# Batch 0: q, k and the shift copied straight from SBUF into the stacks, head by head, and weight folding placed behind the column sums

## The reference

```python
# layer 0: 8 heads of 16, per batch
q, k, v = x @ Wq, x @ Wk, x @ Wv              # split into heads
w = softmax(where(adj > 0, q @ k.T / sqrt(16), -1e9))
x = layernorm(x + (w @ v) @ Wo + bo)
# layer 1
h = x @ W.T
e = (h @ a1)[:, None] + (h @ a2)[None, :]
e = where(e >= 0, e, 0.2 * e)
x = layernorm(x + softmax(where(adj > 0, e, -9e15)) @ h)
```

## Time and profile before

| | us |
|---|---|
| median of 3 runs | 891.87 |
| lowest, highest | 888.39, 896.82 |
| the profiled execution | 889.27 |
| span of its records | 887.3 |
| TensorE busy | 818.8 (92%) |
| ScalarE busy | 702.3 |
| VectorE busy | 698.0 |

### The profile page before, as it was taken

The page is one execution under the profiler, slowest core; times in us unless marked ns, Lnnn a source line. Parts: engine busy times, 40 slices in busy tenths (PEclk is TensorE's granted clock), DMA queues, the critical chain, the costliest instruction groups (busy, mean ns, idle before and its releaser), DMA issues.

```text
span 887.3 us, 19518 instructions
## 1 busy us (share of the span) xinstructions
PE 818.8 (92%) x7647; PEld 400.1 (45%) x7680; DVE 698.0 (79%) x1141; ACT 702.3 (79%) x766; POOL 118.1 (13%) x92
## 2 busy tenths in 40 slices
PE   6399999989999999999999999999999999998982
PEld 4023334425643365334643357333653356433861
DVE  5288679797788978988788977988878987788473
ACT  2399899999779977899779986899769996898050
POOL 4000100030012010031001120132000220122030
PEclk9599999999999999999999999999999999999997
DMA  4656617441266135452365224661363422401001
GB/s 148 147 158 174 132 62 191 152 87 49 96 175 146 39 100 128 129 124 63 106 169 149 37 78 143 156 133 37 107 166 117 90 85 85 96 2 49 1 13 39
DMA packets 51779, 92.16 MB, mean 104 GB/s; under 512 B 3729, under 2 KB 20882, under 8 KB 51666
## 3 DMA queue, kind: packets, MB, share of 16 engines
q1 hardware_dynamic: 51682, 90.85, 38.8%
HBM read 67.63 MB, written 23.20 MB: 102 GB/s over the span
## 4 chain that ended last, share of the span: by engine, by line
PE 69%; ACT 15%; issue 9%; DVE 5%; POOL 0%; POOLq 0%; ACTq 0%; DVEq 0%
PE acc L474 18%; PE slot L509 12%; ACT weights L632 11%; PE slot L441 9%; PE slot L450 9%; PE slot L520 3%; PE slot L446 3%; PE slot L453 2%; ACT atts L658 2%; PE slot L557 2%; DVE x L920 2%; PE slot L571 2%; PE slot L547 2%; PE slot L579 2%; PE slot L491 1%
## 5 line engine op out<-in xcount | busy, mean ns | idle before, releaser
L632 ACT ACTIVATE weights<-slot 128x1024 f32<-128x1024 f32 x504 | 491.8, 1040 | 75.8 <-PE slot L450 38.0
L844 DVE SCALAR_TENSOR_TENSOR weights<-mask,weights 128x1024 f32<-128x1024 bf16 x336 | 403.4, 1236 | 52.8 <-ACT weights L632 42.7
L474 PE MATMUL acc<-weights,vst 128*17 128x512 f32 x2048 | 243.6, 594 | 0.0
L441 PE MATMUL slot<-qst,kst 97*32 97x512 bf16 x2240 | 160.5, 383 | 5.8 <-ACT weights L632 5.2
L450 PE MATMUL slot<-qst,kst 97*128 97x512 bf16 x464 | 133.6, 389 | 25.7 <-issue 13.8
L509 PEld LDWEIGHTS slot<-hst,atts 128*128 128x128 f32 x896 | 106.8, 191 | 17.4 <-ACT weights L632 9.6
L509 PE MATMUL slot<-hst,atts 128*128 128x129 f32 x896 | 110.5, 276 | 3.2 <-issue 1.7
L474 PEld LDWEIGHTS acc<-weights,vst 128*17 128x17 f32 x2048 | 52.3, 97 | 119.8 <-issue 96.8
L441 PEld LDWEIGHTS slot<-qst,kst 97*32 97x32 bf16 x2240 | 49.5, 95 | 116.0 <-ACT weights L632 49.3
L859 DVE SCALAR_TENSOR_TENSOR atts<-turn,hst,mask 128x1024 f32<-128x1024 f32 x64 | 83.2, 1323 | 21.5 <-DMA k_scratch<-atts 15.2
L781 POOL TENSOR_TENSOR rstd<-vareps,exponent 128x4 f32<-128x4 f32 (+1 forms) x24 | 29.3, 1222 | 468.3 <-DVE vareps L915 468.3
(11 more groups left out here) (135 smaller groups left out, 683.5 us busy)
## 6 DMA issues: line engine op xcount, KB each, us to landing
raw<-in_adjT SPq DMA_DIRECT2D x64, 512.0 KB, 3.6
q_scratch<-atts SPq DMA_DIRECT2D x48, 256.0 KB
qst<-q_scratch SPq DMA_DIRECT2D x16, 768.0 KB
k_scratch<-atts SPq DMA_DIRECT2D x24, 256.0 KB
kst<-k_scratch SPq DMA_DIRECT2D x16, 384.0 KB
xT_sb<-in_xT SPq DMA_DIRECT2D x8, 512.0 KB, 4.4
kst<-k_scratch SPq DMA_DIRECT2D x16, 256.0 KB
x_sb<-in_x SPq DMA_DIRECT2D x8, 512.0 KB, 4.7
```

Source lines behind the costliest of these rows:

```text
L441: mm = pe.matmul(ps[rows, cols], kst[:, h, keys], qst[:, h, cols], start=True, stop=not by_pe)
L474: mm = pe.matmul(acc[VW * i:VW * i + HD + 1, cols], vst[b % 2][:, t, g * HG + i], weights[:, HG * buffer(b, n) + i, cols], start=(t == 0), ...
L632: act.activation(to, ps[:], ACT.Exp, scale=SCALE).then_inc(exp_done, 1)
L844: dve.scalar_tensor_tensor(out=to, in0=masks[b % 2][:, n % T], scalar=0.0, in1=at, op0=ALU.is_equal, op1=ALU.mult).then_inc(masked, 1)
```

## The change

For batch 0 alone, nothing goes through DRAM: first_stacks copies each block of each head with one SBUF-to-SBUF transfer (16 rows of 1024 bf16), and the shift of each head with one of a single row. The order is q part 0 and k part 0 of group 0, q parts 1 and 2, k parts 1 and 2, the shift rows of group 0; then all pieces of group 1 and its shift rows. All of it takes the place of the job partsq of batch 0; the other jobs for the parts, the shift and the stacks of batch 0 are empty. From batch 1 on all is as before, with the counts of the semaphores moved and with waits of batch 1's writers of the parts and the shift on the stacks of batch 0. In PE's program fold_second_layer moves from behind k to behind cc; q no longer waits for wk.

```diff
     STACK_DMAS = 5
+    FIRST_DMAS = (2 * BLOCKS + 1) * HG
...
+        def stacks_in(b):
+            return 16 * (FIRST_DMAS + STACK_DMAS * b)
...
                 if b > 0:
                     for g in range(NG):
-                        sp.wait_ge(stack_in[g], b * 16 * STACK_DMAS)
+                        sp.wait_ge(stack_in[g], stacks_in(b - 1))
...
+            def place(s, i, g):
+                for r in range(BLOCKS):
+                    if (QPART, KPART)[s][r] == i:
+                        for h in range(g * HG, (g + 1) * HG):
+                            sp.dma_start((qst, kst)[s][r * HD:(r + 1) * HD, h],
+                                         parts[s][i][h * HD:(h + 1) * HD]).then_inc(stack_in[g], 16)
+
+            def first_stacks():
+                for s in range(2):
+                    sp.wait_ge(part0_made, s + 1)
+                    place(s, 0, 0)
+                for s in range(2):
+                    sp.wait_ge(parts_made, s + 1)
+                    place(s, 1, 0)
+                    place(s, 2, 0)
+                sp.wait_ge(taken["cc"], 1)
+                for h in range(H):
+                    if h == HG:
+                        for s in range(2):
+                            for i in range(3):
+                                place(s, i, 1)
+                    sp.dma_start(qst[KROWS:SROWS, h], negshift[h:h + 1]).then_inc(stack_in[h // HG], 16)
...
             def job(name, me):
-                if name[:3] == "raw":
+                if me == 0 and (name[:5] in ("parts", "stack") or name == "shift"):
+                    if name == "partsq":
+                        first_stacks()
+                elif name[:3] == "raw":
...
-            sp.dma_start(wq[:], Wq).then_inc(wqk_in, 16)
+            sp.dma_start(wq[:], Wq).then_inc(wq_in, 16)
             load_xT(0)
-            sp.dma_start(wk[:], Wk).then_inc(wqk_in, 16)
+            sp.dma_start(wk[:], Wk).then_inc(wk_in, 16)
...
                 if u % (UNITS // NG) == 0:
-                    pe.wait_ge(stack_in[g], (b + 1) * 16 * STACK_DMAS)
+                    pe.wait_ge(stack_in[g], stacks_in(b))
...
                     if me == 0:
-                        pe.wait_ge(wqk_in, 32)
+                        pe.wait_ge(wq_in if name == "q" else wk_in, 16)
...
                     pe.wait_ge(squares_made, 2 * me + 2)
+                    if me == 0:
+                        pe.wait_ge(pool_step, 4)
...
                         job(name, me)
-                        if me == 0 and name == "k":
+                        if me == 0 and name == "cc":
                             fold_second_layer()
...
                 if name in ("q", "k"):
+                    if me == 1:
+                        for g in range(NG):
+                            act.wait_ge(stack_in[g], stacks_in(0))
...
                     act.wait_ge(kmax_made, me + 1)
-                    act.wait_ge(shift_out, me * 16)
+                    if me == 1:
+                        for g in range(NG):
+                            act.wait_ge(stack_in[g], stacks_in(0))
+                    if me > 1:
+                        act.wait_ge(shift_out, (me - 1) * 16)
...
                 dve.wait_ge(parts_made, 2 * b + s)
+                if b == 1:
+                    for g in range(NG):
+                        dve.wait_ge(stack_in[g], stacks_in(0))
```

More of the change, by code:

```diff
@@ L239, in build_fast @@
         acc_read = sem("acc_read")
-        wqk_in = sem("wqk_in")
+        wq_in = sem("wq_in")
+        wk_in = sem("wk_in")
         consts_in = sem("consts_in")
@@ L357, in load_stack @@
                 if what == "q":
-                    sp.wait_ge(parts_out[0], (b + 1) * 96)
+                    sp.wait_ge(parts_out[0], b * 96)
                     sp.dma_start(qst[0:KROWS, heads], q_scratch[heads].rearrange("h i d n -> (i d) h n")).then_inc(stack_in[g], 16)
                 elif what == "k":
-                    sp.wait_ge(parts_out[1], (b + 1) * 48)
+                    sp.wait_ge(parts_out[1], b * 48)
                     for r, n in K_RUNS:
@@ L365, in load_stack @@
                 else:
-                    sp.wait_ge(shift_out, (b + 1) * 16)
+                    sp.wait_ge(shift_out, b * 16)
                     sp.dma_start(qst[KROWS:SROWS, heads], shift_scratch[heads].rearrange("(o h) n -> o h n", o=1)).then_inc(stack_in[g], 16)
@@ L848, in sum_atts @@
                 if j == 0:
-                    dve.wait_ge(parts_out[0], min(b + 3, B) * 96)
-                    dve.wait_ge(parts_out[1], min(b + 3, B) * 48)
+                    dve.wait_ge(parts_out[0], (min(b + 3, B) - 1) * 96)
+                    dve.wait_ge(parts_out[1], (min(b + 3, B) - 1) * 48)
                     dve.wait_ge(full["cc"], min(b + 3, B))
```

## The result

The changed kernel takes 922.39 us (median of 4; 921.97 to 923.14) against 891.38 before: a ratio of 1.0345, 95% interval 1.0316 to 1.0374. It is 31 us slower. The forecast was 905, slower, with a range up to 916: the direction came out, and so did the wait that carries the loss; the size is over twice what was forecast, and outside the range.

What follows compares the result with a forecast made beforehand. The stack load alone was taken to hold unit 0 back, then SyncE's issue ahead of raw 2: 12.6 (mask 2) + 3.0 (clock) = +15.6 on 889.27 gives 904.9, rounded 905 us; range 885 to 916.

Steps and rivals of the forecast that it cites:

- the price of a piece: SyncE's issue of each of batch 0's 96 copies of 16 rows: 0.475 us, ends kept 0.27 and 0.65.
- the near rows: Setup loads and k stack transfers issued right behind each other on SyncE, 0.43 us long, gaps to 0.48, taken as price.
- The 0.30 for the shift's rows: SyncE's issue of each of the 8 single-row shift copies in batch 0, put at 0.30 us.
- The rest of the sum: SyncE free at 57.3, raw 2 lands at 60.9, mask 2 12.6 us later; with 3.0 for the clock, +15.6.
- The clock's term: TensorE idles ahead of mask 2, so what follows starts at 1.2 GHz: 3.0 us more, bounds 0 and 5.
- rival D: Slack later in batch 0 takes up the stall, only the earlier unit 0 stays: 886.7 us; chance 0.03.
- Unit 0: First unit of batch 0, after group 0's pieces: starts at about 35.0 instead of 37.6, 2.6 us won.
- Rival C: Issue is dearer, 0.65 us a piece as for the k stores or with full queues: 921.7 us; chance 0.09.
- Group 1's due time: Group 1's stack in batch 0 is needed at unit 32 only; batch 1's new waits are long met.
- Folding and wk: Setup: folding behind the column sums brings k parts some 2 us earlier, worth nothing; q free of wk: 0.
- Rival A: Short pieces are cheap for SyncE to issue, 0.27 us each: 883.7 us, faster; chance 0.12.
- rival B: Each piece costs SyncE what a load that stands alone does, 0.37 us: 892.6 us, no change; chance 0.19.

Runs made afterwards that it cites:

- both experiments: Folding back behind k in the changed kernel: 923.09 us; folding behind the column sums and q free of wk in the kernel before: 890.96 us.
- the added rows: The kernel before, with back-to-back rows of small transfers of several kinds added to SyncE in the last batch; 913.3 us, one run.

## Why the prediction was wrong

**The step that failed is the price of a piece.** It was put at 0.475 us, "for they go out back to back as the near rows did", and measured 0.63. With the shift's rows (0.30 each, measured 0.63) SyncE's program ended 18.7 us later than worked out: 96 x 0.157 = 15.1 for the pieces, 8 x 0.33 = 2.6 for the rows, 1.1 for one issue that took 1.73, 0.4 for one longer gap (these two make the 16.57 of the timeline), less 0.5 for the earlier start, 18.7 in all. SyncE came free at 76.0 instead of 57.3. The near rows were chosen by their spacing and their size. Size does not matter within SBUF (1 to 64 rows at 0.59); where the two ends lie does, and all near rows had one end in DRAM. The 0.30 for the shift's rows had the same flaw: the rows it was taken from, 0.23 to 0.29, came from DRAM, and stood alone or behind one other.

**The rest of the sum held.** With 76.0 put in, the same steps give 76.0 + 3.6 = 79.6 for mask 2 (measured 79.99) and, with 3.0 for the clock, a loss of 34.3 in the profiled execution (measured 33.9). That the two lie so close is partly luck. The clock's term was 3.0, with bounds of 0 and 5, and behind the stall it measured 1.2 (mask 7 against mask 2); the 1.6 us of the low clock in the last batch, which the prediction does not have, fill most of the difference. A context at 1.2 GHz took 3.62 us, near the "twice" that was estimated. The estimate was too high where it set the cost of the first four units at 2.6: mask 3 follows mask 2 in 4.67 us (84.66 - 79.99) instead of 5.35, and only mask 4 is behind, 10.4 us after mask 2 instead of 9.1. The loss of the stall was passed on in full: rival D falls. One stall, not three, is what the trace has.

**Unit 0** was to start 2.6 us earlier and started 5.2 later. The same price did that: 48 x 0.157 + 4 x 0.33 = 8.9, less 0.5 for the earlier start and 0.7 because unit 0 began 1.2 us behind the last issue and not 1.9, is 7.7 of the 7.8 between the two. (The prediction's own steps add up to 33.3 + 1.9 = 35.2, not 35.0; its sum does not use it.)

**Rival C** (0.65 a piece, 921.7 us) has the number that was measured, at a chance of 0.09, but by luck. It took its price from the k stores and from full queues; here the DMA share was 0.24, and stores of 16 rows cost 0.46. Its bound was in the working, as the upper end of the price, and the range of 885 to 916 cut it off. The price was the one number on which all hung, 104 times, and at 104 us of time for each us of price the range should have reached to the price's upper bound, 922.

**Group 1's due time** was a second error, hidden in the changed kernel, so that it took nothing from the forecast. "It is needed at unit 32 only" and "the new waits of batch 1 on the first stacks are long met" are both wrong: q's job of batch 1 stands at position 19. In the changed kernel the stall at mask 2 covers it; with raw 2 moved, 12.8 us of it show.

**Folding and wk** were put at nothing, and both experiments agree. **Rival A** would have needed a price under 0.34, and **rival B** 0.37. Such prices were seen only for a load that stands alone or follows one other (0.33, 0.29); in the added rows, loads and stores came at 0.46 and copies within SBUF at 0.63.

**Not settled:** why a copy within SBUF costs SyncE more than one with an end in DRAM; why a single issue now and then takes 1.5 to 1.7 us (one of the 104, and one of six in two of the added rows); and why the k stores took 0.65 with their gaps, and the six q stores 1.02 on average, when stores of 16 rows take 0.46. The stores' other shape (8 heads outermost) and size (256 KB) were not tried by themselves.

## What to carry to other kernels

Before replacing one big transfer by many small ones, multiply their number by what one costs its queue, and take that price from a transfer with the same ends. Of two small transfers that were alike otherwise, the copy within SBUF was the dearer here (0.63 against 0.46), and a round trip through DRAM in few transfers was quicker than the direct way in many. Then read on in the same queue's program: the first thing behind the new transfers that an engine needs sets the loss, not the data that they carry. And a buffer that is read by late copies is due when its next writer comes, which may be long before its reader does.

## What the runs showed of the hardware

- Issue by SyncE of a small transfer in a row of like ones: 0.42 us (0.46 with the gap) with one end in DRAM (stores of 16 rows, loads of 16 and 32), 0.59 (0.63) with both in SBUF, there the same for 1, 16, 32 and 64 rows of 2 KB and for 2- and 4-byte types. The first of a row took 0.31 or 0.33 as a load, 0.50 as a store, and within SBUF 0.49 to 0.53, once 0.63. Stores of 256 KB with 8 heads outermost took 0.57 to 1.4 each.
- Now and then a single issue takes 1.5 to 1.7 us; this is one of a row of six copies within SBUF:

```profile
819.95 1.58 SPq L397 DMA_DIRECT2D xT_sb<-xT_sb  x1
```

- Loads of blocks from DRAM beside their stores kept the DMA engines at a share of 0.94 to 1.07 at only 162 to 196 GB/s; 96 copies of 32 KB within SBUF, one behind another, left them at 0.24 and 52 GB/s.
